# Second attention with expanded queries and 32-row score tiles, keys first, shared layer norm, halved end

## The reference

```
sublayer 0  q = xn Wq, k = ctx Wk, v = ctx Wv      8 heads of 64, 154 context rows
            x += softmax(q k^T / 8) v Wo + bo
sublayer 1  scores = sigmoid(xn Wg); 2 of 4 groups, then 4 of 16 experts of width 64, plus a shared one
            x += sum_e c_e (silu(xn W1e) * (xn W3e)) W2e + shared
sublayer 2  q = xn Wq, k = ctx Wk, v = ctx Wv      16 heads of 8, 154 context rows
            x += softmax(q k^T / sqrt(8)) v Wo
sublayer 3  softmax router, 2 of 8 experts of width 256, plus a shared one
            x += sum_e c_e (silu(xn W1e) * (xn W3e)) W2e + shared
```

## Time and profile before

| | |
|---|---|
| three runs | 249.87, 250.09, 250.65 us (median 250.09) |
| the profiled execution | 250.26 us, of which the span of instructions is 247.6 us |
| TensorE busy | 235.8 us (95% of the span) |
| TensorE weight load | 177.6 us (72%) |
| VectorE busy | 173.4 us (70%) |
| ScalarE busy | 162.6 us (66%) |
| GpSimd busy | 119.2 us (48%) |

### The profile page before, as it was taken

The page is one execution under the profiler, slowest core; times in us unless marked ns, Lnnn a source line. Parts: engine busy times, 40 slices in busy tenths (PEclk is TensorE's granted clock), DMA queues, the critical chain, the costliest instruction groups (busy, mean ns, idle before and its releaser), DMA issues.

```text
span 247.6 us, 4720 instructions
## 1 busy us (share of the span) xinstructions
PE 235.8 (95%) x1426; PEld 177.6 (72%) x1426; DVE 173.4 (70%) x478; ACT 162.6 (66%) x387; POOL 119.2 (48%) x110
## 2 busy tenths in 40 slices
PE   6799999999999999998899999999999999999993
PEld 2476765964888888897666674768687788887872
DVE  3339993698557834679998996576788555865782
ACT  3749979888669376531498967873758745655560
POOL 1503745889039597991300171003890923838440
PEclk9689999999999999999799999999999999999999
DMA  7850000000059808603100000009000064000002
GB/s 225 247 220 0 5 0 3 3 0 1 3 132 320 275 10 208 134 0 128 69 0 4 5 0 5 0 4 308 33 0 1 3 186 156 0 3 1 0 0 85
DMA packets 7069, 17.18 MB, mean 69 GB/s; under 512 B 1492, under 2 KB 2101, under 8 KB 6663
## 3 DMA queue, kind: packets, MB, share of 16 engines
q1 hardware_dynamic: 6822, 16.58, 21.9%
q10 hardware_dynamic: 224, 0.32, 0.4%
HBM read 16.21 MB, written 0.62 MB: 68 GB/s over the span
## 4 chain that ended last, share of the span: by engine, by line
PE 76%; DVE 9%; DMA 7%; issue 3%; ACT 3%; SPq 2%; POOL 0%; DVEq 0%; ACTq 0%; POOLq 0%
PE psum L1050 10%; PE psum L1051 9%; PE psum L1053 9%; DMA w_src<-in_w 5%; PE psum L1202 4%; PE psum L1120 4%; PE psum L1236 3%; PE psum L1252 3%; PE psum L1209 3%; PE psum L1281 3%; PE psum L1211 3%; PE psum L1210 3%; PE psum L1162 3%; PE psum L1153 3%; PE psum L1131 2%
## 5 line engine op out<-in xcount | busy, mean ns | idle before, releaser
L640 POOL TENSOR_TENSOR act_s<-act_s,spread 128x512 f32<-128x512 f32 x48 | 60.8, 1293 | 46.6 <-DMA spread<-cw 25.1
L1050 PE MATMUL psum<-xT_hi,w_hi 128*128 128x512 f32 x108 | 44.6, 413 | 0.4 <-ACT act_s L728 0.4
L1053 PE MATMUL psum<-xT_lo,w_hi 128*128 128x512 f32 x108 | 42.7, 395 | 0.0
L1051 PE MATMUL psum<-xT_hi,w_lo 128*128 128x512 f32 x108 | 42.5, 394 | 0.0
L728 ACT ACTIVATE act_s<-psum 128x512 f32<-128x512 f32 x54 | 31.4, 599 | 15.6 <-PE psum L1053 10.7
L895 DVE TENSOR_TENSOR q<-psum,q 128x512 fp32r<-128x512 f32 x36 | 24.8, 689 | 17.4 <-ACT q L738 17.0
L738 ACT CAST q<-psum 128x512 fp32r<-128x512 f32 x36 | 21.1, 585 | 21.1 <-PE psum L1211 15.4
L1018 DVE TENSOR_REDUCE neg_max<-psum 128x2 f32<-128x308 f32 x64 | 26.4, 470 | 1.6 <-PE psum L1236 1.5
L997 DVE TENSOR_TENSOR psum<-psum,act_s 128x512 f32<-128x512 f32 x36 | 24.1, 692 | 3.2 <-PE psum L1053 1.6
L688 ACT ACTIVATE prob<-psum,neg_max 128x154 f32<-128x154 f32 x64 | 24.0, 412 | 2.9 <-DVE neg_max L864 2.7
L615 POOL TENSOR_TENSOR prob_n<-prob,row_inv 128x1024 f32<-128x1024 f32 x8 | 15.2, 1898 | 21.6 <-DVE row_inv L871 19.7
(11 more groups left out here) (150 smaller groups left out, 477.8 us busy)
## 6 DMA issues: line engine op xcount, KB each, us to landing
spread<-cw SPq DMA_DIRECT2D x16, 256.0 KB, 5.3
spread<-cw SPq DMA_DIRECT2D x8, 512.0 KB, 5.4
w_src<-in_w SPq DMA_DIRECT2D x2, 1152.0 KB, 5.2
w_src<-in_w SPq DMA_DIRECT2D x1, 2304.0 KB, 12.6
w<-in_w SPq DMA_DIRECT2D x1, 576.0 KB, 6.6
X<-in_x SPq DMA_DIRECT2D x2, 256.0 KB, 4.2
wq_src<-in_wq SPq DMA_DIRECT2D x2, 256.0 KB, 5.4
out<-X SPq DMA_DIRECT2D x2, 256.0 KB, 2.0
```

The source lines that it names most:

```text
L640: pool.tensor_tensor(g, g, spread[:, slot, :], ALU.mult).then_inc(weighed, 1)
L1050: pe.matmul(dst, w_hi, xT_hi[:, b, :], start=True, stop=False)
L1051: pe.matmul(dst, w_lo, xT_hi[:, b, :], start=False, stop=False)
L1053: return pe.matmul(dst, w_hi, xT_lo[:, b, :], start=False, stop=True)
```

## The change

1. **Queries of the second attention.** `wq1` is now loaded with its 128 real columns only. A step `qd` for each batch multiplies once (three matmuls) and is rounded by ScalarE and split by VectorE. A step `q1` then expands all four groups with eight matmuls on 32-row tiles of a 0/1 matrix `sel`: the first four copy hi into the first and third place of each head, the second four add lo in the second place. ScalarE copies the four results (`q1copy`). `sel` is built on VectorE at the start.
2. **Transposed scores.** An `expT` step now covers four heads: four matmuls, each over the 32 rows of one head, at four tile positions and into four banks. TensorE waits for all four banks ahead of the first. The exponential is a step `exp` of its own for each head.
3. **Layer norm.** ScalarE writes tiles 0 and 1, GpSimd tiles 2 and 3. TensorE transposes in the order 0, 2, 1, 3.
4. **Start.** The keys of sublayer 0 stand ahead of the transposes; `wv0` is loaded before the second half of x.
5. **End.** `ycopy`, `yT`, `res` and `out` of sublayer 3 are done by halves of a batch.
6. **Second feed-forward.** The rounded `w2_1` has a place of its own instead of the keys' `k1`, and its split no longer waits for the last `expT`.
7. **Order.** All five strings of `PROGRAM` are new.

```diff
-wq_src1, wq_hi1, wq_lo1 = split_pair("wq1", [P, G1 * P])
+wq_src1, wq_hi1, wq_lo1 = split_pair("wq1", [P, H1 * DH1])
+sel = sb("sel", [P, 2, 4, 4, DH1], F32R)
...
-            load(wq_src1[:, :], a["wq1"], "wq1")
+            load(wq_src1[:, :].rearrange("k (h d) -> k h d", d=DH1),
+                 a["wq1"].rearrange("k (h c) -> k h c", c=PAD)[:, :, 0:DH1], "wq1")
...
+                    pool.wait_ge(rstd_ready, 2 * position[step])
+                    for t in (2, 3):
+                        pool.tensor_scalar(xn[:, b, t, :], X[:, b * T + t, :], rstd[:, b, t:t + 1], shift[:, b, t:t + 1],
+                                           ALU.mult, ALU.add).then_inc(xn_ready[1], 1)
...
-                    for t in range(T):
+                    for t in (0, 1):
                         act.activation(xn[:, b, t, :], X[:, b * T + t, :], ACT.Identity,
...
-                elif kind == "q1":
...
-                    act.copy(rounded[:, g % 2, :], bank(step)).then_inc(q1_rounded, 1)
+                elif kind == "qd":
...
+                    act.copy(qd[:, 0, :], bank(step)).then_inc(qd_rounded, 1)
+                elif kind == "q1copy":
+                    b, g = step[1:]
+                    wait_filled(act, ("q1", b, g))
+                    moved(act.copy(q1[:, b, g, :], bank(("q1", b, g))), ("q1", b, g))
...
-                    dve.wait_ge(q1_rounded, position[step])
-                    moved(dve.scalar_tensor_tensor(q1[:, b, g, :], rounded[:, g % 2, :].bitcast(F32), lo_rows[:, 0:1],
-                                                   bank(step), ALU.mult, ALU.add), step)
+                elif kind == "sel":
+                    dve.wait_ge(loaded["ident"], 16)
+                    settle()
+                    note(dve.memset(sel[:, :, :, :, :].bitcast(F32).rearrange("p k j s d -> p (k j s d)"), 0.0))
+                    note(dve.tensor_reduce(sel_sum[:, :], ident[:, :].rearrange("p (g c) -> p c g", g=4), AX, ALU.add))
...
+                elif kind == "qd":
...
+                    moved(dve.tensor_tensor(qd[:, 1, :], bank(step), qd[:, 0, :].bitcast(F32), ALU.subtract), step)
...
                 elif kind == "q1":
-                    c = slice(g * P, (g + 1) * P)
-                    filled(product3(bank(step), wq_hi1[:, c], wq_lo1[:, c], 2, b), step)
+                    for part in range(2):
+                        if part == 1:
+                            wait_moved(pe, ("qd", b))
+                        for g in range(G1):
+                            rows = slice(PAD * g, PAD * g + PAD)
+                            ins = pe.matmul(bank(("q1", b, g)), sel[rows, part, :, :, :].rearrange("p j s d -> p (j s d)"), qd[rows, part, :],
+                                            start=(part == 0), stop=(part == 1), skip_group_check=True, tile_position=(PAD * g, 0))
...
                 elif kind == "expT":
-                    filled(pe.matmul(bank(step), k1[:, b, g, j, 0:P], q1[:, b, g, :], start=True, stop=True), step)
+                    for j in range(4):
+                        wait_bank_free(pe, step + (j,))
+                    for j in range(4):
+                        rows = slice(PAD * j, PAD * j + PAD)
+                        filled(pe.matmul(bank(step + (j,)), k1[rows, b, g, j, 0:P], q1[rows, b, g, :], start=True, stop=True,
+                                         skip_group_check=True, tile_position=(PAD * j, 0)), step + (j,))
...
     "SP":
-        "store spread spread spread fetch spread store spread spread spread spread fetch place_max place_max " +
+        "store spread spread spread spread fetch store spread spread spread spread fetch place_max place_max " +
```

More of the change, by code:

```diff
@@ L112, in all_steps @@
     steps += [("weigh", s, b, i) for s in (1, 3) for b in batches for i in range(N_SHARED[s], N_HID[s])]
-    steps += hidden("hsplit", (3,)) + per_sublayer("ycopy", (3,)) + per_sublayer("yT", (3,))
+    steps += hidden("hsplit", (3,))
+    for kind in ("ycopy", "yT", "res"):
+        steps += [(kind, 3, b, half) for b in batches for half in range(2)]
     for kind in ("k1", "place_k1s"):
@@ L117, in all_steps @@
     steps += [("place_k1", g, j) for g in groups for j in range(4)]
-    for kind in ("vf1", "onT", "wo1"):
+    steps.append(("sel",))
+    for kind in ("vf1", "qd", "q1", "onT", "wo1"):
         steps += per_batch(kind)
@@ L204, in takes @@
     if engine == "PE":
-        return kind != "score"
-    if kind == "scores":
+        return True
+    if kind in ("scores", "q1", "expT"):
         return False
@@ L228, in bank_uses @@
 def bank_uses():
-    uses, count = {}, {}
+    uses, count, last = {}, {}, {}
     for step, token in zip(order_of("PE"), PROGRAM["PE"].split()):
@@ L238, in bank_uses @@
             keys = [("pv1", step[1], g) for g in REST_SETS[step[2]]]
+        elif kind == "q1":
+            keys = [("q1", step[1], g) for g in range(G1)]
+        elif kind == "expT":
+            keys = [step + (j,) for j in range(4)]
         else:
@@ L242, in bank_uses @@
             count[bank] = count.get(bank, 0) + 1
-            uses[key] = (bank, count[bank])
+            uses[key] = (bank, count[bank], last.get(bank))
+            last[bank] = key
     return uses
@@ L513, in _ @@
             load(ident[:, :], a["ident"], "ident")
+            load(wv0[:, :], a["wv0"], "ctxv")
             load(X[:, T:2 * T, :], a["x"][:, T:2 * T, :], "x1")
-            load(wv0[:, :], a["wv0"], "ctxv")
             for r in ROW_PARTS:
@@ L739, in _ @@
                 elif kind == "ycopy":
-                    b = step[2]
+                    b, half = step[2:]
+                    at = slice(2 * P * half, 2 * P * half + 2 * P)
                     wait_filled(act, ("y", 3, b))
-                    wait_filled(act, ("wo1", 1) if b == 0 else ("yT", 3, 0))
-                    moved(act.copy(yT[:, :], bank(("y", 3, b))), ("y", 3, b))
+                    wait_filled(act, ("wo1", 1) if b == 0 else ("yT", 3, 0, half))
+                    ins = act.copy(yT[:, at], bank(("y", 3, b))[:, at]).then_inc(y_copied, 1)
                 elif kind == "k1":
```

179 lines of the change are left out of this document (104 added, 75 removed), and 55 rows, old and new, of the table PROGRAM.

## The result

Four runs of the changed kernel took 241.28 to 242.51 us, median **241.72 us**; the kernel before took 250.37 us in four runs. The ratio is 0.967, with an interval of 0.964 to 0.970: 3.3% faster. The profiled execution took 242.51 us and spans 239.7 us, 7.9 less than before.

The account below looks back on a forecast made before the run. TensorE was taken to bound the kernel, with VectorE also at its limit in the second attention. 250.3 - 3.2 - 2.7 - 2.4 + 0.8 - 0.5 = 242.3, less 0.2 for the median: 242 us, range 236.5 to 248.5.

Parts of the forecast that it names:

- likeliest case: Whole kernel: the forecast of 242 us itself, own range 239.5 to 245 us, chance 0.52.
- Start, 3.2 us: Kernel start: keys fill TensorE's gap ahead of the transposes; 3.2 us less, middle of 2.0 (half clock) and 4.6 (full).
- End of the first feed-forward, 2.7 us: Up to 114 us: TensorE does 2.1 us less work, and fewer mixed `down` blocks save 0.6; 2.7 us less.
- Tiles: Transposed scores: four matmuls on row tiles run nearly side by side, 0.50 us a group with shape changes, instead of 0.93.
- Second attention, 2.4 us: Residual of batch 1 to last sublayer's first hidden tile: 0.6 less to the statistics, the rest behind them; 2.4 us less.
- This is VectorE's sum: Second attention to the next statistics: VectorE's 34.8 us of work plus 1.7 us of waiting set the time, 36.5 us.
- Statistics to first hidden tile: Ahead of the last sublayer, 7.4 us before: shared norm saves 0.8 us, and a `rest1` of 1.0 us moves behind.
- The work moved behind, 0.8 us more: Last sublayer: the moved `rest1` of 1.0 us comes back, less 0.2 for cheaper scores; 0.8 us more.
- End, 0.5 us: Kernel end: copy, transposes and addition become overlapping halves; 0.5 us less, between 0.1 and 0.9.
- Serial tiles and a clock at half: Rival, second attention: row tiles run one after another and the clock is half as often as full; 253.5 us, chance 0.07.
- Grouped banks: Rival: waiting for four free banks costs six groups 0.5 us each, and the start gives 2.0; 246.3 us, chance 0.18.
- Everything lands: Rival: full clock at the start, VectorE never waits in the second attention, tiles side by side; 238.5 us, chance 0.20.

Follow-up runs that it names:

- slow layouts: Changed kernel with 128, 1920 or 64 unused bytes behind `hid`, which moves the weights' addresses: 242.95, 242.52 and 243.34 us.
- gap of 1024 bytes: Changed kernel with 1024 unused bytes behind `hid` in SBUF, so the weights lie 896 bytes before their old address: 241.46 us.

## Why the prediction came out right, and where it was wrong

The time was 242 predicted, 241.72 measured, within the likeliest case's own range. That it came so close is luck: the start gave 0.7 us less than its term and the second attention up to the first hidden tile 2.1 less, while the end of the first feed-forward gave 1.0 more and the last sublayer 1.8 more.

**Start, 3.2 us.** The mechanism was right: keys in the gap, no fall of the clock, first query at 10.47 where 10 to 12.5 was forecast. Alone it was worth 2.3 to 2.5 us, between the bounds of 2.0 and 4.6. Keys first alone gave 1.4 us; with another bank, the value product and the earlier `wv0` it was 2.3, and which of the three matters was not tried. The middle of two bounds was 0.7 us too high.

**End of the first feed-forward, 2.7 us.** The residual of batch 1 is 6.2 us earlier; less the start's 2.5 that is 3.7 for this step, 1.0 more than forecast. With the norm on ScalarE alone this residual came 1.0 later, so the surplus has the size of the gain at the norms, which the forecast put at 0; the addresses give 0.2 (97.8 us from the first query to this residual in the slow layouts, 97.6 in the changed kernel). The parts of this step itself were not tried alone. The sum of both terms, 5.9, was good to 0.3.

**Tiles.** The four `expT` matmuls start within 0.01 us of each other, where 0.3 us was the sign to look for, and the group takes 0.43 us where 0.50 was taken. So the tiles do run side by side. By the Trainium skill (TensorE: Matmul & The Clock Gate, Measured speedup vs the span model) an estimate for the group is 0.30; the trace lies between the two. In the 0.43 is the change of shape behind the group; the Trainium skill (TensorEngine Tiling (Array Packing), Key Properties) warns of such changes. Putting the zeros back cost 3.2 us in the result. An expansion takes 0.67 us from its start to the next step's (119.83 to 120.50), 0.8 taken.

**Second attention, 2.4 us.** This is the step that failed: "This is VectorE's sum". The sum gave 36.5 us, and it took 38.5. VectorE's work was about right: 34.8 us by the sum's prices, and the trace has it busy for 35.5. What was too small is the time beside it, 1.7 us in the sum and 3.7 by the same prices: 2.1 up to the first `od` copy (21.8 us for 19.7 of work), 1.5 from there to the residual (14.4 for 12.9), and 0.1 at the statistics.

In the second of these parts TensorE sets the time. It is busy for all of the 14.42 us, and with VectorE relieved to 10.3 us the part still takes 14.3, with 14.0 of work on TensorE where I had put 12.9. In the first part TensorE has 15.5 us of work, not 12.9, but that is still far under 21.8; and with 6.6 us taken from VectorE it got only 0.8 shorter. Mostly chains set the time there: TensorE waits for the copy of the queries, the layer norm, and the maxima's way into `rows`, and most of 1.06 us of work put there was free. What was mis-sized is thus TensorE's work, 25.8 us in the sum and 29.5 measured, because I counted each matmul at the distance inside a row of its own kind. The kind changes 47 times in this stretch, and where it does more time passes: four `score1` take 0.76 us behind the 32-row tiles, not 4 x 0.14 = 0.56. The 3.7 us by which the sum was short on TensorE are 0.08 for each change; that they all lie in the changes is not shown. The half clock took little of it: 3.4 us at half cost 0.25.

Taking 10 us from VectorE won 1.1; giving TensorE 4.5 cost 3.2. My sign to look for, VectorE over 93% busy with gaps on TensorE, was met only up to 120 us (11.48 of 12.10); behind it is 91% for VectorE against 97% for TensorE. The first hidden tile of the last sublayer came at 152.33 instead of near 150.5.

**Statistics to first hidden tile.** 5.8 us, 5.6 forecast. The norm tile on GpSimd takes 0.45 us where 0.40 was taken, next to ScalarE's in the lines of both:

```profile
L625 POOL TENSOR_SCALAR xn<-X,rstd,shift 128x128 f32<-128x128 f32 x16 | 7.0, 449 | 0.8
L690 ACT ACTIVATE xn<-X,shift,rstd 128x128 f32<-128x128 f32 x16 | 7.0, 487 | 4.1 <-POOL shift L622 4.1
```

"At the other norms ... their gain is 0" was wrong: without the shared norm the kernel took 2.0 us more in all, 1.5 to 1.8 at the same clock, and 0.6 of it came at the start.

**The work moved behind, 0.8 us more.** It became 1.0 less, 1.8 off. Half of that is the addresses: the smaller `wq1` and the new `sel` moved the weights by 1920 bytes, and at the old addresses the stretch takes 83.7 us instead of 82.8. None of my terms or rivals held this. The other 0.9 us, from 0.8 more to 0.1 less than before, stay unexplained. At the old addresses the kernel took 243.07 us, still in the range, and the forecast would have been a little too low instead of level.

**End, 0.5 us.** 0.4 measured, two halves are copied in 0.65 us, and the transposes start 0.52 us after the first copy did:

```profile
235.54 0.65 ACT L772 COPY onT<-psum 128x256 f32<-128x256 f32 x2 [1.85 <-PE psum L1258]
```

**Rivals.** Serial tiles and a clock at half for more than 7 us did not come (about 3.4 us at half). Grouped banks did not show as a wait ahead of `expT`. The second attention, though, lost 2.0 of the 3 us that rival had for it, for another reason. "Everything lands" had its full clock at the start, but not a VectorE that never waits.

No kernel tried beats the changed one beyond what can be told, save the one that leaves half the columns out of the maximum. The one with a gap of 1024 bytes took 241.46 us, the same within the runs' spread.

## What to carry to other kernels

Where two engines are both over 90% busy, price the work of each with the changes between kinds of instruction, and not only with the distance inside a row; on TensorE the sum by distances was 3.7 us short over 47 changes. Then ask of each what it would win alone: two short runs, one easing VectorE and one burdening TensorE, help to decide it, read part by part: here one part was TensorE's, and another neither's. And after an edit that changes the size of a tile, compare the distance of equal matmuls before looking for reasons in the order: every later tile has moved.

## What was not expected of the hardware

- The distance of 512-column float32r matmuls depends on where their operands start in SBUF: 0.228 us at two places 128 bytes off a step of 256 (counted from the old address), 0.2315 to 0.2322 at three others. For the hidden tiles it is the weights' address, since their moving operand stayed where it was; for the second product it was not told apart, since `q1`, from which it reads, moves with its weights.
- The clock fell to half at 7.7 us in the kernel before, in a pause of 2.56 us, and held at full in all profiled executions with the keys first, whether TensorE paused for 1.5 us ahead of the queries or not. With that pause the runs spread over 3.3 us at mean clocks from 0.982 to 1.000. Idle time alone doesn't tell when it falls: after 0.71, 0.49 and 0.92 us of it between 108 and 115 us it fell in the changed kernel (below), and with half the maximum, after 0.71, 0.80, 1.50 and 1.36, it did not:

```profile
115.00:117.50 2.50, 2.21 (x6) 1.87 (x7) 2.50 (x8) 0.52 (x2) 1.29 (x1) 0.50 0.00 0
```

- Four float32r matmuls of 512 columns on row tiles of 32, each into its own bank, start within 0.01 us and took 0.43 us to the start of the next step, against 0.99 for the four over all rows.
